# A graph attention layer and a quantised linear layer: sums per window of 32 nodes in column strips, with the last stage placed between the gathers

## What is computed

```
h   = layernorm(x)
xp  = (h @ W).reshape(N, 4, 256)                  # 4 heads
e   = leaky_relu(a_src[src] + a_dst[dst])         # with a self loop for each node
ee  = exp(e - segment_max(e, dst)[dst])
z   = segment_sum(ee, dst)
gnn = relu(segment_sum(xp[src] * (ee / z[dst]), dst) + bias)
x1  = x + gnn
xq  = quantise(layernorm(x1))                     # blocks of 32 on a 6-bit grid, times their scale
out = x1 + xq @ quantise(ffn_weight).T + ffn_bias
```

## Time and profile before

| | |
|---|---|
| time, median of 3 runs | 1360.31 us (1359.4, 1360.31, 1364.32) |
| profiled execution, span | 1363.2 us (its own time is not listed apart; it is nearest to the run of 1364.32) |
| `normalise` | 0 to 129.3 us |
| `project` | 131.1 to 465.5 us |
| `aggregate` | 465.5 to 1052.3 us |
| `finish` | 1052.5 to 1363.2 us |
| busy share of the span | TensorE 94%, DVE 79%, ACT 72%, POOL 55% |

### The profile page before, as it was taken

One profiled execution on the slowest core, in us unless ns is written; L12 is line 12 of the kernel. 1 busy time (PEld: TensorE's weight loads), 2 busy tenths in 40 slices (PEclk: granted clock), 3 DMA queues, 4 the chain that ended last, 5 costly groups with the idle time before them and its releaser, 6 DMA issues. The chain is left out here.

```text
span 1363.2 us, 29337 instructions
## 1 busy us (share of the span) xinstructions
PE 1276.4 (94%) x10053; PEld 895.9 (66%) x10053; DVE 1070.2 (79%) x2221; ACT 988.2 (72%) x2239; POOL 747.8 (55%) x677
## 2 busy tenths in 40 slices
PE   7898888999999789999999899999996799999997
PEld 5776444554445378888888788888886344455543
DVE  6998899889844478888888788888885977777771
ACT  3666888884456388998888899899995566666661
POOL 1000766661247377777777777777772344444441
PEclk9899999999999899999999999999999899999999
DMA  7785586543454689999999999999998577777743
GB/s 260 248 301 191 167 309 193 187 154 133 153 210 171 245 323 381 378 368 361 376 360 380 394 401 375 375 336 369 376 369 314 158 192 190 188 191 189 190 101 53
DMA packets 111554, 361.54 MB, mean 265 GB/s; under 512 B 22108, under 2 KB 22892, under 8 KB 111156
## 3 DMA queue, kind: packets, MB, share of 16 engines
q0 software_dynamic: 68192, 225.42, 47.8%
q1 hardware_dynamic: 39860, 133.38, 28.1%
q10 hardware_dynamic: 3360, 0.91, 0.2%
HBM read 297.76 MB, written 72.82 MB: 272 GB/s over the span
## 5 line engine op out<-in xcount | busy, mean ns | idle before, releaser
L1800 PE MATMUL sum_ps<-xg,wgt 128*128 128x256 f16 x4992 | 561.4, 273 | 18.5 <-DMA xg<-d_xp,tables 10.7
L1771 ACT ACTIVATE wgt<-hot,tables 128x128 f16<-128x128 f16 x1664 | 503.1, 388 | 73.4 <-DVE hot L1715 63.2
L1800 PEld LDWEIGHTS sum_ps<-xg,wgt 128*128 128x128 f16 x4992 | 472.5, 98 | 75.3 <-DMA xg<-d_xp,tables 11.8
L1696 POOL DMA_INDIRECT xg<-d_xp,tables x404 | 418.0, 1035 | 127.5 <-issue 119.0
L1569 PE MATMUL xp_ps<-acc 128*128 128x512 f16 x1152 | 263.1, 381 | 8.2 <-DVE acc L1122 5.6
L1755 DVE TENSOR_TENSOR acc<-sum_ps,acc 128x1024 f32 x220 | 268.9, 1222 | 1.1 <-issue 1.0
L2198 PE MATMUL fmm_ps<-xg,tables 128*128 128x512 f16 x1200 | 263.1, 379 | 1.4 <-DVE tables L2027 1.4
L2198 PEld LDWEIGHTS fmm_ps<-xg,tables 128*128 128x128 f16 x1200 | 117.4, 98 | 137.8 <-issue 1.9
L1569 PEld LDWEIGHTS xp_ps<-acc 128*128 128x128 f16 x1152 | 109.3, 98 | 129.3 <-issue 4.9
L1726 DVE TENSOR_TENSOR wgt<-hot,tables 128x512 f16<-128x512 f16 x416 | 157.6, 418 | 0.0
L1929 POOL TENSOR_TENSOR tables<-tables,finv 128x1024 f32<-128x1024 f32 x24 | 45.9, 1914 | 131.8 <-DVE finv L2015 131.8
(11 more groups left out here) (328 smaller groups left out, 1586.7 us busy)
## 6 DMA issues: line engine op xcount, KB each, us to landing
d_xnT<-acc SPq DMA_DIRECT2D x25, 512.0 KB, 3.6
own_row<-d_own SPq DMA_DIRECT2D x25, 512.0 KB, 5.6
wdT<-in_x_dram SPq DMA_DIRECT2D x24, 512.0 KB, 4.9
acc<-d_xnT SPq DMA_DIRECT2D x24, 512.0 KB, 5.2
d_xp<-acc SPq DMA_DIRECT2D x24, 512.0 KB, 3.0
d_own<-acc SPq DMA_DIRECT2D x24, 512.0 KB, 4.3
xr<-in_x_dram SPq DMA_DIRECT2D x24, 512.0 KB, 6.7
out_dram<-acc SPq DMA_DIRECT2D x24, 512.0 KB, 6.7
```

Of the source, the lines that this page charges most:

```text
L1696: nc.gpsimd.indirect_dma_start(out=xg[s][u][:, :, :].rearrange("p a n -> p (a n)"), out_offset=None, in_=d_xp, in_offset=bass.IndirectOffs ...
L1771: last = nc.scalar.activation(wgt[k % WB][:, u, h, :], hot[k % TURN][:, u, :], ACT.Copy, scale=col(numT[:, h, :], u, q))
L1800: last = nc.tensor.matmul(sum_ps[s][:, h * C:(h + 1) * C], w[:, u, a * HEADS + h, :], x[u][:, b, h * C:(h + 1) * C], start=(u == 0 and h % ...
```

## The change

- **Windows.** Sums are made per window of 32 nodes (98 windows) and not per tile of 128. There are 488 slots, one group of 128 edges each (391 groups, and 97 more for groups that reach into another window). In `sums` the four heads of a window lie in four blocks of 32 partitions, 256 columns and 2 for the sums of the numerators (AW = 258).
- **Strips.** Per slot TensorE does 12 matmuls with a stationary matrix of 32 columns, each into 32 partitions of the same bank (head h into strip h), then 4 of 2 columns.
- **Weights.** VectorE makes one-hots of 32 columns for 4 slots at a time and, per slot, all 8 products (256 columns). ScalarE makes none.
- **Order.** `normalise` sorts the tiles by their number of slots and makes the table that gives for each slot its first edge group and window: the chain of small DVE operations after the histogram becomes longer. `order_i` holds the sorted order.
- **Last stage between the gathers.** `aggregate` and `finish` become `gather_and_finish`. READY[r] is the slot behind which tile r counts as complete (every 20 or 21 slots). Each step of the last stage has a fixed offset in slots from READY[r]: on DVE mix +1, x1 +9, root +11, scales +13, rescale +15, low +18, final +30; on TensorE the 8 transposes +16 and the 48 matmuls in chunks of 5 behind each slot from +18 to +27. There is one buffer `mm_ps`, `tr_ps`, `own_row`, `xqT`. The division and multiplication with the scales move from POOL to DVE, the accumulating output DMA is gone (`final` on DVE, then one store by SP). ScalarE moves the four heads of a tile from strips back to rows (`move`, 16 operations of 32x256).
- **Smaller edits.** `wdT` stays in SBUF (no `d_wd`), `numT` is gone, all gathers share the bound in one register, and finished tiles of `acc` serve as further gather buffers (6, later 11).

```diff
-            for k in range(XB, STEPS):
-                gather(k)
+            bound = nc.gpsimd.to_reg(NP - 1)
+            for k in range(SLOTS_ALL):
+                gather(k)
...
+            def weights(p):
+                if p >= WB:
+                    dve.wait_ge(slot_done, PAIR * (p - WB + 1))
+                dve.wait_ge(hot_ready, p // 2 + 1)
+                for u in range(PAIR):
+                    k = PAIR * p + u
+                    last = nc.vector.tensor_tensor(out=wgt[p % WB][:, u, :, :].rearrange("p v (n b) -> p v n b", b=2),
+                        in0=hot[k // HOTS % HB][:, k % HOTS, :].rearrange("p (n b) -> p n b", b=2).unsqueeze(1)
+                        .to_broadcast([P, V, WIN // 2, 2]),
+                        in1=numT16[:, k, :, :].unsqueeze(2).to_broadcast([P, V, WIN // 2, 2]), op=ALU.mult)
+                last.then_inc(wgt_ready, 1)
+            def add(k):
+                w = dve.value_load(tile_row[0:1, k:k + 1], min_val=0, max_val=WINS - 1)
+                dve.wait_ge(slot_done, k + 1)
+                if k >= 1:
+                    dve.wait_ge(added, k)
+                to = sums[:, bass.ds(w, 1), :].rearrange("p o n -> p (o n)")
+                nc.vector.tensor_tensor(out=to, in0=sum_ps[k % SB][:, 0:AW], in1=to, op=ALU.add).then_inc(added, 1)
...
+            for k in range(SLOTS_ALL):
+                if k % PAIR == 0:
+                    p = k // PAIR + AHEAD
+                    if p % 2 == 0 and p // 2 * HOTS < SLOTS_ALL:
+                        one_hots(p // 2)
+                    if p * PAIR < SLOTS_ALL:
+                        weights(p)
+                if k == 0:
+                    dve.wait_ge(cleared, 3)
+                add(k)
+                for turns, do in due:
+                    for r in turns.get(k + 1, ()):
+                        do(r)
...
+            def slot(k):
+                j, s, p, u = PLACES[k][0], sum_ps[k % SB], k // PAIR, k % PAIR
+                if u == 0:
+                    pe.wait_ge(wgt_ready, p + 1)
+                pe.wait_ge(arrived[j], landed[k])
+                if k >= SB:
+                    pe.wait_ge(added, k - SB + 1)
+                for i, (a, b) in enumerate(((0, 0), (0, 1), (1, 0))):
+                    for h in range(HEADS):
+                        nc.tensor.matmul(s[h * WIN:(h + 1) * WIN, 0:C], wgt[p % WB][:, u, a * HEADS + h, :], xg[j][:, b, h * C:(h + 1) * C],
+                                         start=(i == 0), stop=(i == 2), skip_group_check=True)
+                for h in range(HEADS):
+                    last = nc.tensor.matmul(s[h * WIN:(h + 1) * WIN, C:AW], hot[k // HOTS % HB][:, k % HOTS, :], numT16[:, k, h:V:HEADS, 0],
+                                         start=False, stop=True, skip_group_check=True)
+                last.then_inc(slot_done, 1)
...
+            for k in range(SLOTS_ALL + MULTIPLY_AT + len(every)):
+                if k < SLOTS_ALL:
+                    slot(k)
+                for r in turns.get(k + 1, ()):
+                    turned(r)
+                for r, first, behind in chunks.get(k + 1, ()):
+                    products(r, first, behind)
```

1056 lines of the change are left out of this document (435 added, 621 removed).

## The result

The changed kernel takes 1547.62 us (median of 4 runs, 1545.75 to 1549.79) where the kernel before takes 1359.86 in the same comparison: 1.137 times as long, 95% interval 1.135 to 1.139. The forecast was 1443, at most 1520. Its direction was right, it was 105 us short, and the time lies outside its range.

A forecast was written before the change was run, and what follows sets the result against it. TensorE bounds the kernel before; in the merged stage TensorE and VectorE take turns. Adds begin at 495, plus 56 for first slots, 823 for 22 periods, 5 and 66: 1445 us span, predicted 1443, range 1300 to 1520.

The forecast's parts named there:

- Rivals 1: Merged stage: POOL and DMA set the pace, 26.7 us per tile, some 1190 us in total; chance 0.08.
- 2 (VectorE alone, 31.2 us): Merged stage: VectorE alone bounds, TensorE's chunks hidden under it, period 31.2 us, total 1308 us; chance 0.14.
- 3 (strips one after another): TensorE's slots: strips do not overlap, 1.48 us per slot, period 47 us, total about 1675 us; chance 0.08.
- the period: Time per tile in the merged stage: 36.6 us plus 0.8 for the clock, 37.4 us, taken 22 times, 823 us.
- VectorE waits for the transposes: Merged stage, once per tile: VectorE waits for transposes (1.04 us) and one slot, holding one slot in hand: 1.1 us.
- phase 2: Part of each tile that VectorE sets: forecast 10.3 slots at 0.90 us plus 10.0 us of steps, 19.3 us.
- I take 0.90 us, near the lower end: VectorE's time per slot in the merged stage, queue included: mean 0.885, at most 1.0, taken as 0.90 us.
- rival 4: Clock falls in each tile and one-hot wait holds the queue: +1.0 +3.2 us per tile, 1515 us; no separate chance.
- I take half of the tiles: +0.8: TensorE starting at its low clock after idling loses about 1.6 us; counted in half the tiles, +0.8 us per tile.
- Phase 1: Part of each tile that TensorE sets: forecast 10 chunks of 1.10 us and 10 slots of 0.5 us, 16.0 us.
- the tail: End of the merged stage, one tile behind the other in single buffers, through the last store: 66 us.
- my floor of 0.55: TensorE's slot: 16 matmuls at 0.034 us cannot come under 0.55 us if issue sets it; 0.5 us was taken.

The follow-up runs named there:

- filler_all: Changed kernel plus six constant 128x512 matmuls behind each of eight slots per tile and twelve behind slot 17: 1512.4 us, 1.112 of the kernel before.
- chunk3: Changed kernel with last-stage products in 16 chunks of 3, not 10 of 5, and final at slot 36, not 30: 1624.4 us (kernel before 1564.5), ratio 1.039.
- turn19: Changed kernel with transposes behind slot 19, not 16, low at 19, first products at 20, final at 32: 1471.4 us, 1.080 of the kernel before.

## Why the prediction was wrong

**What held.** The chain behind the histogram is 18 us long (128.25 to 146.3), as forecast, and the stage begins at 481.2 (480.5). The first add is at 496.5 (495), the first phase of TensorE begins at 554.5 (551). `project` kept its time. The register is worth nothing. GpSimd and DMA wait for slots. The add is 0.426 us, the steps of a tile without mix come to about 9.5 us by the gaps between adds (10.0), a chunk with its slot 1.63 (1.60). TensorE and VectorE do take turns, and this makes the kernel slower. Rivals 1 (GpSimd sets the pace), 2 (VectorE alone, 31.2 us) and 3 (strips one after another) did not happen.

**What failed is the period:** 41.4 us for 37.4, times 22, which is 87 of the 103 us. Cut at the last product, the forecast reads 15.1 us for 48 products and nine slots and 0.8 for the clock, and 21.5 for the rest. Measured are 17.35 and 24.03. Three terms were too small:

1. *"VectorE waits for the transposes (1.04 us) and one slot while it has one slot in hand: 1.1 us."* The wait is 1.95 us on average (2.24 in the tile shown), since the transposes and the slot behind them run at the low clock. And its worth is larger than its length: with the order changed so that VectorE has slots in hand, phase 2 fell by 3.3 us. I took the clock into account for the chunks and forgot it for the transposes, which start 6 us ahead of them.
2. *"I take 0.90 us, near the lower end."* Bare slots take 1.04. The largest part of this is the wait for the one-hots that holds the queue (1.54 and not 1.05), which I had priced and then left to rival 4. 11.3 x 0.14 = 1.6 us per tile. The reason that I gave, that the queue ran ahead of the engine in the earlier trace rows, was read off a stretch where an add of 1.2 us covered it.
3. *"I take half of the tiles: +0.8."* The clock falls in every tile, and the first products meet it low in 21 of 22. Phase 1 takes 15.5 us at full clock (filler_all) and 17.35 as it is, so it loses 1.85. TensorE is nearly idle ahead of the transposes, as the window 915 to 922.6 shows.

Beyond the forecast they are 0.85 + 1.6 + 1.05 = 3.5 of the 4.0 us. Phase 1 at the full clock is another 0.4 longer than forecast (15.5 for 15.1), and the steps of a tile are 0.5 shorter; this is a sum of means, not exact to the last tenths. Rival 4 named terms 2 and 3 together, and it was the right case, but it lacked the first term and its figure does not follow from its own terms: +1.0 and +3.2 over 22 tiles give 1535 and not 1515 (1518 if the 3.2 takes the place of the 0.8), and the 3.2 is worked out nowhere. The prediction's own loss of 1.6 us per start, in all tiles and not half of them, gives +0.8, and with the +1.0 some 1483 us. Another 12 us are in the tail (83.3 for 71; the items that the prediction lists for it come to about 63 and not to its 66), where the last products run partly at the low clock as well: 48 of them take 12.9 us, 40 take 10.9 and then 8 take 3.2.

The other 3.5 us are in the first slots, up to the first product (554.5 for 551). The range failed because I treated the clock and the queue as chances that come out one way or the other by halves. Each followed from something that the forecast itself said: TensorE idle for most of the second phase, one-hots ahead of the products in every fourth slot. Once these are certain, the upper end becomes the likeliest value, and the range has to reach beyond it.

**Strips and the change of shape.** The slot of 0.355 us is shorter than my floor of 0.55, which took 0.034 us from one row of 32-column matmuls as the least distance of any matmuls. Sixteen here take 0.022 each: strips that use different columns overlap. The Trainium skill (TensorE: Matmul & The Clock Gate, Part 3) gives 2.38 times for three column strips; here four gain more, 1.48 / 0.355 = 4.2 times against one after another by my sum. On the switch of shapes: a chunk with its slot takes 1.63, the parts 5 x 0.215 + 0.355 = 1.43, and in chunk3 1.20 for 3 x 0.215 + 0.355 = 1.00, so a chunk's two switches cost 0.20 us at either size, 2 us per tile with ten chunks. The Trainium skill (TensorEngine Tiling (Array Packing), "Key Properties") says that a change of mode drains the engine; the trace agrees as far as a loss at each change goes, and this is its price. (The section "Instruction Overhead", which the prediction names beside it, says nothing of this.) It was hidden in my 0.5 for the slot, too large by 0.15.

**What stays open.** What slowed three of the five groups; whether the register helps in them; how the gain of turn19 (3.3 us) splits between the wait itself (1.95 to 0.33 us) and the slot that moved behind `low`; and the full price of the clock, of which filler_all shows 35 us.

## What to carry to other kernels

When two engines in fixed orders share a stage, count at each hand-over how many pieces the waiting engine has in hand, and price the engine that has been idle at its low clock from its first operation on. Here another order mended the first (turn19, 5% for two lines of constants), and filler matmuls into a bank that nobody reads at the time mended most of the second (filler_all, 2.3%).

A step that becomes short brings its queue to light. What cost nothing under an operation of 1.2 us (a table load of 0.30, a check of 0.21, a wait that holds the queue for 0.5) set the pace under one of 0.43; one load for several steps, without its checks, gave 3.6%.
